# Rebuilding the first layer norm of an eight-stage transformer kernel, and the order of its start

## The chip, the cores and the metric

The kernel runs on one core of a Trainium2 chip. The metric is the device time of one launch in microseconds (us), as the median of several runs; the profile is one more execution, taken with the hardware profiler.

## The reference

Eight stages work in turn on `x` (8 batches x 128 tokens x 512 numbers); each adds its result to `x` after a layer norm. There are four cross-attentions over the same context `ctx_4096` and four feed-forward networks. What the change touches is the beginning, stage 0:

```python
def _layernorm(x, axis=-1, eps=1e-05):
    m = jnp.mean(x, axis=axis, keepdims=True)
    v = jnp.var(x, axis=axis, keepdims=True)
    return (x - m) / jnp.sqrt(v + eps)
...
        x = _rmsnorm(hidden_states, ln_weight)      # x * rsqrt(mean(x*x) + EPS) * weight
        h_q = (x @ w_q.T).reshape(b, lq, H, DH)     # H = 32 heads, DH = 128
        h_k = (key_value_states @ w_k.T).reshape(b, lk, H, DH)
        h_v = (key_value_states @ w_v.T).reshape(b, lk, H, DH)
        score = jnp.einsum('bqhd,bkhd->bhqk', h_q, h_k)
        score = score + position_bias[None]
        ...
        attn = jnp.einsum('bhqk,bkhd->bqhd', score, h_v).reshape(b, lq, H * DH)
        out = attn @ w_out.T
        return hidden_states + out
...
    x = x + _L0_xattn_ref(_layernorm(x, axis=-1), ctx_4096, ...)
```

So the normalised `x` is used twice in stage 0: scaled once more by the root of its own mean square as the input of the queries, and added unscaled to `x`.

## The kernel before

All matrices are fp32 values that are split in two fp32r parts, a "high" copy and a "low" remainder, and each product is three matmuls (high x high, high x low, low x high; `PASSES`). The context is held transposed as `ctxT[:, 0 or 1, chunk, token]`, the normalised activations as `xnT` in the same form, with 1024 tokens and four chunks of 128 features. Weights come in tiles of 128x512 (256 KB) through a ring of four slots, `ring`, and are split into `w_kv`, `w_kv2`, `w_in` and `w_out`. POOL makes both parts (L651 high, L653 low).

Each engine runs its own instruction list, in the order in which it is written out; semaphores tie them together. Stage 0 runs 32 heads in 8 groups of 4; group 0 and the last group are written out, the six between are a loop (`Fori`). The attentions of stages 4 (`LA[2]`) and 6 (`LA[3]`) have such loops too.

The start of the kernel, before any loop:

- SP queues (`start_sp`) the constants, half of `x` (batches 0 to 3, 1 MB), four 256 KB pieces of the context into the ring, the other half of `x`, the mask, and four more context pieces, each of which has to wait until POOL has split an earlier piece out of the same ring slot. Only then come two loads for a later stage (`F0_b`) and the first weights: key, value, value, query of head 0, key and query of head 1 (`attention_sp`).
- ACT copies each context piece to the high part (L2163), POOL subtracts for the low part (L2170), 8 pieces each.
- DVE (`dve_tail(dve, 0, None)`) takes the statistics of each batch (L437, L439). After four batches it computes the reciprocal root of the variance by Newton steps (`dve_rsqrt`, L409 to L419, 11 tiny operations) and then a second root for the mean square. This chain of some 26 operations runs twice, once for each half of the batches (`dve_ln_rstd`). It then norms each batch in three passes (`dve_ln_norm`): L467 subtracts the mean and scales, L471 adds the result to `x`, L473 scales by the second root. Four buffers (`tbuf`, `pbuf`) hold normed batches.
- PE turns a normed batch (four 128x128 transposes, L484) into one of four banks, ACT copies it out (L494), and DVE makes the low part (L507).
- PE's own order is: turns of batches 0 to 3, keys of head 0 (two halves of 12 matmuls of 128x512), values of the pair of heads 0 and 1 (four fills of 24 matmuls of 128x256, alternating between the banks `proj0` and `proj1`), turns 4 to 7, queries of head 0 (two halves), scores, keys and queries of head 1, and then the steady order of group 0. ACT empties `proj0` (L952), DVE empties `proj1` (L955).

Ahead of stage 4's attention DVE executes 32 waits on a semaphore that was reached long before (`DVE_ALIGN`, L2269).

Of the kernel before, what the change touches and what calls it, by code (L numbers as in the profile page):

```python
# [7 lines left out]
F32 = mybir.dt.float32  # L8
# [19 lines left out]
DVE_ALIGN = 32  # L28
# [228 lines left out]
def build(nc, ins, out):  # L257

    with ExitStack() as ctx:
# [61 lines left out]
        with nc.sbuf_tensor("low_a2", [P, 11 * 96], F32R) as low_a2, nc.sbuf_tensor("low_b2", [96, D], F32R) as low_b2:  # L321
# [22 lines left out]
        ctx_split = sem("ctx_split")  # L344
# [3 lines left out]
        ln_stats, ln_moments, ln_shifted, ln_newton, ln_rstd, ln_normed, ln_full, ln_high, ln_low, ln_rms, ln_kept = (  # L348
            sem(f"ln_{n}") for n in "stats moments shifted newton rstd normed full high low rms kept".split())
# [77 lines left out]
        ln_calls = [0]  # L427
        LN_STAGES = [0, 1, 3, 4, 5, 6, 7]
# [4 lines left out]
        def dve_ln_stats(dve, n, b):  # L433

            if n == 0 and b % BH == 0:
                dve.wait_ge(x_landed[b // BH], 16)
            dve.bn_stats(stats[:, b, :], x[:, b, :]).then_inc(ln_stats, 1)  # L437
            dve.wait_ge(ln_stats, 8 * n + b + 1)
            dve.bn_aggr(moments[:, b, :], stats[:, b, :]).then_inc(ln_moments, 1)  # L439

        def dve_ln_rstd(dve, n, half):
# [7 lines left out]
            if n == 0:  # L449

                dve.scalar_tensor_tensor(rrms[:, cols], rstd[:, cols], 1.0, rstd[:, cols], ALU.mult,
                                         ALU.mult).then_inc(ln_rms, 1)
                dve.wait_ge(ln_rms, 3 * half + 1)
                dve.tensor_tensor(rrms[:, cols], rrms[:, cols], moments[:, cols, 1], ALU.mult).then_inc(ln_rms, 1)
                dve.wait_ge(ln_rms, 3 * half + 2)
                dve.tensor_scalar(nw_v[:, cols], rrms[:, cols], EPS, None, ALU.add).then_inc(ln_rms, 1)
                dve.wait_ge(ln_rms, 3 * half + 3)
                dve_rsqrt(dve, rrms[:, cols], nw_v[:, cols], nw_t[:, cols], ln_shifted, ln_newton, ln_calls[0])
                ln_calls[0] += 1

        def dve_ln_norm(dve, n, b):
# [6 lines left out]
            if n == 0:  # L468
                norm.then_inc(ln_kept, 1)
                dve.wait_ge(ln_kept, 2 * b + 1)  # L470
                dve.tensor_tensor(x[:, b, :], x[:, b, :], out_ap, ALU.add).then_inc(ln_kept, 1)  # L471
                dve.wait_ge(ln_kept, 2 * b + 2)
                dve.tensor_scalar(out_ap, out_ap, rrms[:, b:b + 1], None, ALU.mult).then_inc(ln_normed, 1)  # L473
            else:
                norm.then_inc(ln_normed, 1)
# [11 lines left out]
        def act_ln_high(act, n, b):  # L487
# [4 lines left out]
            if n == 0:  # L492
                for c in range(DC):
                    a = act.activation(xnT[:, 0, c, b * S:(b + 1) * S], src[:, c, :], ACT.Copy,  # L494
                                       scale=vecs[:, V_LNW + c:V_LNW + c + 1])
            else:
                a = act.activation(xnT[:, 0, :, b * S:(b + 1) * S], src, ACT.Copy)
            a.then_inc(ln_high, 1)

        def dve_ln_low(dve, n, b):  # L500
# [4 lines left out]
            if n == 0:  # L505
                for c in range(DC):
                    a = dve.scalar_tensor_tensor(xnT[:, 1, c, b * S:(b + 1) * S], src[:, c, :],  # L507
                                                 vecs[:, V_LNW + c:V_LNW + c + 1],
                                                 xnT[:, 0, c, b * S:(b + 1) * S].bitcast(F32), ALU.mult, ALU.subtract)
            else:  # L510
                a = dve.tensor_tensor(xnT[:, 1, :, b * S:(b + 1) * S], src, xnT[:, 0, :, b * S:(b + 1) * S].bitcast(F32),  # L511
                                      ALU.subtract)
            a.then_inc(ln_low, 1)
# [26 lines left out]
        def pe_tail(pe, n, out_of):  # L540
            for b in range(B):
                if out_of:
                    out_of(b)
# [7 lines left out]
            for A in LA.values():  # L551
                if A.stage == n:
                    if n == 0:
                        pe.wait_ge(ctx_split, 8)
                    for what in "kv":
                        project_head(pe, A, 0, 0, what)
# [23 lines left out]
        def dve_tail(dve, n, add_of):  # L580
# [3 lines left out]
            early = BH if add_of else BH - 1  # L584
            for b in range(B):
                if add_of:
                    add_of(b)
# [27 lines left out]
        def attention_sp(sp, A):  # L615
# [20 lines left out]
            for what, _, j in A.first:  # L636
                load(0, j, what)
            group(0)
# [4 lines left out]
        def attention_pool(pool, A):  # L643
# [130 lines left out]
        def project_values(pe, A, g, j):  # L774
# [4 lines left out]
            for fill in range(4):  # L779
# [8 lines left out]
        def project_head(pe, A, g, j, what, squares=None):  # L788
# [11 lines left out]
            for half in range(2):  # L800
# [188 lines left out]
        def attention_act(act, A):  # L989
# [65 lines left out]
            exps(0, 0, 1)  # L1055
            if A.normed:
# [27 lines left out]
        def attention_dve(dve, A):  # L1084
# [75 lines left out]
            def add(p, b):  # L1160
                m.wait(dve, "added", B * p + (b - B + 1))
# [982 lines left out]

        def start_sp(sp):
            sp.dma_start(consts[:, :], ins["consts"]).then_inc(consts_landed, 16)
            sp.dma_start(vecs[:, :], ins["vecs"]).then_inc(consts_landed, 16)
            for n in range(8):
                if n % 4 == 0:
                    sp.dma_start(x[:, n:n + 4, :], ins["x"][:, n:n + 4, :]).then_inc(x_landed[n // 4], 16)  # L2150
                if n == 4:
# [227 lines left out]
```

## Time and profile before

| | |
|---|---|
| median of 3 runs | 3134.81 us (3134.13 to 3142.85) |
| the profiled execution, device time | 3132.72 us |
| its span, first to last instruction | 3130.9 us |
| PE busy, share of the span | 94% |
| mean granted TensorE clock | 0.982 |
| matmuls | 16224 |

In the rows below "PE" is the matmul side of TensorE, "PEld" its weight loads, DVE VectorE, ACT ScalarE, POOL GpSimd, SPq the queue of SyncE that issues transfers. A line such as L388 is a line of the kernel. Brackets at the end of a timeline row give the idle time of the engine before the row, and what ended it. A busy matmul row has a modelled end, so rows of PE can overlap a little.

### The profile page before, as it was taken

How to read it: one execution, taken by the hardware profiler on the slowest of the kernel's cores; microseconds unless marked ns; L12 is line 12 of the kernel's file. 1: busy time of each engine (PE TensorE's matmuls, PEld its weight loads, DVE VectorE, ACT ScalarE, POOL GpSimd, SP SyncE). 2: the span in 40 equal slices, each digit the busy share in tenths (PEclk: the TensorE clock that was granted, in tenths of full speed). 3: DMA queues.
4: the chain of work that ended last, by engine and by line, in shares of the span. 5: the costliest groups of instructions: out<-in, count | busy, mean ns of one | idle time of the engine just before them, and what ended most of it. 6: DMA issues, size and time to landing. Idle time of an engine off the chain costs nothing.

```text
span 3130.9 us, 47838 instructions
## 1 busy us (share of the span) xinstructions
PE 2952.5 (94%) x16224; PEld 2501.3 (80%) x16224; DVE 1794.2 (57%) x3625; ACT 1038.1 (33%) x3466; POOL 991.2 (32%) x842
## 2 busy tenths in 40 slices
PE   4999999999989989889989999999889999999899
PEld 4788888888877857768778888888768888888687
DVE  7454444444462258878766666666774444544744
ACT  2222222222222217622144444444313333333332
POOL 3424233333313236533331333222213333332221
PEclk9999999999999999989999999999999999999999
DMA  2111111111111110011110111001011111110111
GB/s 90 58 40 47 39 46 39 46 30 51 40 35 54 33 35 29 26 32 39 42 35 21 34 33 33 27 24 33 24 34 38 39 41 38 33 33 20 44 47 44
DMA packets 69141, 119.75 MB, mean 38 GB/s; under 512 B 8745, under 2 KB 14249, under 8 KB 68641
## 3 DMA queue, kind: packets, MB, share of 16 engines
q1 hardware_dynamic: 69026, 118.26, 12.6%
q8 instruction: 67, 1.10, 0.1%
q14 instruction: 48, 0.39, 0.0%
HBM read 116.06 MB, written 2.10 MB: 38 GB/s over the span
## 4 chain that ended last, share of the span: by engine, by line
PE 82%; DVE 11%; ACT 3%; issue 2%; DMA 0%; DVEq 0%; ACTq 0%; SPq 0%
PE proj L388 39%; PE outp L388 22%; PE heado L905 6%; PE score L872 4%; PE turn L892 2%; PE score L388 2%; DVE stats L437 1%; PE outp L1789 1%; DVE x L1163 1%; PE score L1374 1%; DVE xnT L511 1%; ACT sq L1000 1%; ACT tbuf L1012 1%; PE heado L1789 1%; ACT acts L1033 1%
## 5 line engine op out<-in xcount | busy, mean ns | idle before, releaser
L388 PE MATMUL outp<-w_out,acts 128*128 128x512 f32 x3288 | 847.7, 403 | 20.8 <-DVE x L1163 12.3
L388 PE MATMUL proj<-xnT,w_in 128*128 128x512 f32 x3288 | 783.7, 394 | 8.4 <-DVE xnT L511 2.7
L388 PEld LDWEIGHTS proj<-xnT,w_in 128*128 128x128 f32 x3288 | 613.2, 189 | 139.1 <-issue 6.0
L388 PEld LDWEIGHTS outp<-w_out,acts 128*128 128x128 f32 x3288 | 600.9, 190 | 149.4 <-DVE x L1163 17.4
L388 PE MATMUL proj<-ctxT,w_kv 128*128 128x512 f32 x1536 | 368.7, 396 | 5.8 <-ACT big L952 5.1
L1163 DVE TENSOR_TENSOR x<-x,outp 128x512 f32<-128x512 f32 x384 | 260.9, 684 | 189.1 <-PE outp L388 187.3
L651 POOL TENSOR_TENSOR w_out<-ring,consts 128x512 fp32r<-128x512 f32 x96 | 102.0, 1063 | 840.5 <-PE outp L388 840.5
L388 PEld LDWEIGHTS proj<-ctxT,w_kv 128*128 128x128 f32 x1536 | 285.4, 189 | 71.5 <-ACT big L952 9.4
L955 DVE COPY big<-proj 128x512 f32<-128x512 f32 x136 | 93.6, 689 | 361.7 <-PE proj L388 361.5
L651 POOL TENSOR_TENSOR w_kv<-ring,consts 128x512 fp32r<-128x512 f32 x96 | 100.4, 1046 | 486.8 <-DMA ring<-in_L_wk 463.2
L1187 DVE TENSOR_TENSOR acts<-heado,acts 128x512 fp32r<-128x512 f32 x192 | 132.8, 691 | 175.2 <-ACT acts L1033 175.2
L905 PEld LDWEIGHTS heado<-ptbuf,big 128*128 128x128 f32 x1536 | 201.5, 192 | 30.7 <-ACT ptbuf L1031 15.8
L1033 ACT ACTIVATE acts<-heado 128x512 fp32r<-128x512 f32 x192 | 115.1, 599 | 325.0 <-PE heado L905 325.0
L905 PE MATMUL heado<-ptbuf,big 128*128 128x128 f32 x1536 | 205.1, 277 | 12.5 <-ACT ptbuf L1031 7.2
L952 ACT ACTIVATE big<-proj 128x512 f32<-128x512 f32 x136 | 80.6, 593 | 401.8 <-PE proj L388 400.3
L1031 ACT ACTIVATE ptbuf<-turn 128x512 f32<-128x512 f32 x192 | 114.4, 596 | 267.8 <-PE turn L892 267.8
L388 PE MATMUL proj<-w_kv,ctxT 128*128 128x256 f32 x1536 | 188.9, 284 | 6.6 <-DVE big L955 6.6
L388 PEld LDWEIGHTS proj<-w_kv,ctxT 128*128 128x128 f32 x1536 | 187.7, 191 | 8.4 <-DVE big L955 7.2
L872 PEld LDWEIGHTS score<-big 128*128 128x128 f32 x1536 | 183.2, 192 | 9.0 <-issue 4.4
L872 PE MATMUL score<-big 128*128 128x128 f32 x1536 | 187.2, 275 | 3.0 <-issue 1.7
L1510 DVE TENSOR_TENSOR x<-x,outp 128x512 f32<-128x512 f32 x168 | 115.2, 686 | 105.9 <-PE outp L388 105.6
L651 POOL TENSOR_TENSOR w_in<-ring,consts 128x512 fp32r<-128x512 f32 x96 | 106.6, 1111 | 158.2 <-PE proj L388 157.8
(248 smaller groups left out, 4049.1 us busy)
## 6 DMA issues: line engine op xcount, KB each, us to landing
ring<-in_L_wq SPq DMA_DIRECT2D x96, 256.0 KB, 2.7
ring<-in_L_wo SPq DMA_DIRECT2D x96, 256.0 KB, 2.7
ring<-in_F_in SPq DMA_DIRECT2D x52, 256.0 KB, 2.7
ring<-in_L_wk SPq DMA_DIRECT2D x48, 256.0 KB, 2.7
ring<-in_L_wv SPq DMA_DIRECT2D x48, 256.0 KB, 3.3
ring<-in_F_out SPq DMA_DIRECT2D x41, 256.0 KB, 2.6
x<-in_x SPq DMA_DIRECT2D x2, 1024.0 KB, 7.4
ring<-in_ctxT SPq DMA_DIRECT2D x8, 256.0 KB, 4.8
```

What stands on the lines that cost most here:

```text
L388: mm = pe.matmul(bank_ap, w_ap(a, c), rhs(b, c), start=first and c == 0 and n == 0, stop=last and c == chunks - 1 and n == len(PASSES) - 1)
L651: pool.tensor_tensor(dst[:, slot, 0, :], ring[:, r, :], zeros512, ALU.add).then_inc(m["high_w"], 1)
L872: mm = pe.matmul(score[half][:, b * P:(b + 1) * P], qT[:, t], kT[:, t], start=True, stop=True)
L892: mm = pe.transpose(turn[:, b * P:(b + 1) * P], probs[j % 2][:, half, b * P:(b + 1) * P], ident)
L905: mm = pe.matmul(heado[:, b * P:(b + 1) * P], v_pair[:, n, j % 2, :] if A.own_kv else v[:, n * S:(n + 1) * S], ptbuf[:, half, b * P:(b + 1 ...
L952: return engine.activation(dst, src, ACT.Copy)
L955: return engine.tensor_copy(dst, src)
L1031: act.activation(ptbuf[:, half, :], turn[:, :], ACT.Copy).then_inc(m["tfree"], 1)
L1033: act.activation(acts[:, j, 0, half * HALF:(half + 1) * HALF], heado[:, :], ACT.Copy)\
L1163: dve.tensor_tensor(x[:, b, :], x[:, b, :], outp[b % 2][:, :], ALU.add).then_inc(m["added"], 1)
L1187: dve.tensor_tensor(acts[:, j, 1, cols], heado[:, :], acts[:, j, 0, cols].bitcast(F32), ALU.subtract)\
L1510: dve.tensor_tensor(x[:, b, :], x[:, b, :], outp[b % 2][:, :], ALU.add).then_inc(m["added"], 1)
```

## The change

The start is written anew, in four functions of its own (`start_sp`, `start_pe`, `start_act`, `start_dve`), and the special cases for stage 0 leave the shared layer-norm helpers.

- The context goes to a free buffer (`big`) in four loads of 512 KB that wait for nothing; both halves of `x` and the first weights are queued right behind, the `F0_b` loads and the mask after weights. POOL splits five of the eight context pieces, DVE three.
- ACT makes the high parts of the first three weight tiles (key, value, value), which POOL did.
- The two roots are computed once for all eight batches, with their work tiles in a PSUM bank (`outp[0]`). The two scalings are multiplied into one, so a norm is one pass: even batches on DVE, odd ones on ACT, into eight buffers. The turns use six banks.
- `x = x + norm(x)` becomes one ACT pass for each batch (`x * keep + shift`), behind the exponentials of the first scores; the first additions to `x` (L1163) wait for it.
- PE does keys, value fill 0, turns 0 to 3, fill 1, turns 4 and 5, fill 2, turns 6 and 7, fill 3, queries.
- A tiny ACT operation ahead of the first copies brings the activation table load forward. The 32 waits ahead of stage 4 leave.

```diff
-            for _ in range(DVE_ALIGN):
-                dve.wait_ge(consts_landed, 32)
...
             def split(g, j, what, dst, slot):
...
-                m.wait(pool, ("landed", r), 16 * A.landing(g, j, what))
-                pool.tensor_tensor(dst[:, slot, 0, :], ring[:, r, :], zeros512, ALU.add).then_inc(m["high_w"], 1)
+                if not (A.own_kv and isinstance(g, int) and g == 0 and (what, 0, j) in A.first[:3]):
+                    m.wait(pool, ("landed", r), 16 * A.landing(g, j, what))
+                    pool.tensor_tensor(dst[:, slot, 0, :], ring[:, r, :], zeros512, ALU.add).then_inc(m["high_w"], 1)
...
             exps(0, 0, 1)
+            if A.own_kv:
+                act.wait_ge(ln_rms, 7)
+                for b in range(B):
+                    act.activation(x[:, b, :], x[:, b, :], ACT.Identity, bias=nw_t[:, b:b + 1], scale=nw_v[:, b:b + 1])\
+                       .then_inc(ln_kept, 1)
...
             def add(p, b):
+                if A.own_kv and isinstance(p, int) and p == 0:
+                    dve.wait_ge(ln_kept, b + 1)
...
+        CTX_POOL, CTX_DVE = (0, 1, 2, 4, 6), (3, 5, 7)
...
         def start_sp(sp):
             sp.dma_start(consts[:, :], ins["consts"]).then_inc(consts_landed, 16)
             sp.dma_start(vecs[:, :], ins["vecs"]).then_inc(consts_landed, 16)
+            sp.dma_start(x[:, 0:BH, :], ins["x"][:, 0:BH, :]).then_inc(x_landed[0], 16)
+            for n in range(4):
+                sp.dma_start(big[:, n, :], ins["ctxT"][:, n, :]).then_inc(ctx_landed[n], 16)
+            sp.dma_start(x[:, BH:B, :], ins["x"][:, BH:B, :]).then_inc(x_landed[1], 16)
+
+        def start_pe(pe):
...
+            pe.wait_ge(ctx_split, len(CTX_POOL))
+            pe.wait_ge(ctx_split_dve, len(CTX_DVE))
+            project_head(pe, A, 0, 0, "k")
+            project_values(pe, A, 0, 0, fills=[0])
+            for b in range(4):
+                turn_first(b)
+            project_values(pe, A, 0, 0, fills=[1])
+            for b in range(4, 6):
+                turn_first(b)
+            project_values(pe, A, 0, 0, fills=[2])
+            for b in range(6, 8):
+                turn_first(b)
+            project_values(pe, A, 0, 0, fills=[3])
+
+        def start_act(act):
...
+            for r, dst in enumerate((w_kv[:, 0, 0, :], w_kv[:, 1, 0, :], w_kv2[:, 1, 0, :])):
+                A.events.wait(act, ("landed", r), 16)
+                act.activation(dst, ring[:, r, :], ACT.Copy).then_inc(A.events["high_w"], 1)
+            take_projection(act, True, A, 0, 0, "k")
+            norm_first(1)
+            norm_first(3)
+            high_first(0)
+            take_values_fill(act, True, A, 0, 0, 0)
+            high_first(1)
+            norm_first(5)
+            norm_first(7)
+            for b in range(2, 6):
+                high_first(b)
+            take_values_fill(act, True, A, 0, 0, 2)
+            for b in range(6, 8):
+                high_first(b)
...
+            mean, var = moments[:, :, 0], moments[:, :, 1]
+            arg, work = outp[0][:, 0:B], outp[0][:, B:2 * B]
+            dve.wait_ge(ln_moments, B)
+            dve.tensor_scalar(arg, var, EPS, None, ALU.add).then_inc(ln_rstd, 2)
+            dve.wait_ge(ln_rstd, 2)
+            dve_rsqrt(dve, rstd[:, :], arg, work, ln_shifted, ln_newton, 0)
+            dve.tensor_tensor(work, rstd[:, :], rstd[:, :], ALU.mult).then_inc(ln_rms, 1)
...
+            dve_rsqrt(dve, rrms[:, :], arg, work, ln_shifted, ln_newton, 1)
+            keep, shift = nw_v, nw_t
+            dve.tensor_tensor(rrms[:, :], rrms[:, :], rstd[:, :], ALU.mult).then_inc(ln_rms, 1)
...
+            dve.scalar_tensor_tensor(shift[:, :], rrms[:, :], -1.0, mean, ALU.mult, ALU.mult).then_inc(ln_rms, 1)
...
+            norm_first(0)
+            norm_first(2)
+            take_projection(dve, False, LA[0], 0, 0, "k")
+            norm_first(4)
+            norm_first(6)
...
+            for b in range(2):
+                low_first(b)
+            take_values_fill(dve, False, LA[0], 0, 0, 1)
+            for b in range(2, 7):
+                low_first(b)
+            take_values_fill(dve, False, LA[0], 0, 0, 3)
+            low_first(7)
```

## Rows read from the trace of the kernel before

**Rows 1.** The page: busy shares, and the chain that ended last.

```profile
PE 2952.5 (94%) x16224; PEld 2501.3 (80%) x16224; DVE 1794.2 (57%) x3625; ACT 1038.1 (33%) x3466; POOL 991.2 (32%) x842
...
PE 82%; DVE 11%; ACT 3%; issue 2%; DMA 0%; DVEq 0%; ACTq 0%; SPq 0%
```

**Rows 2.** Waits, 0 to 90 us: total us, times, longest.

```profile
PE turn L484 <- DVE tbuf L473: 26.1, 1, 26.1
```

**Rows 3.** Timeline of the start: start us, us, engine, line, what.

```profile
7.91 0.70 DVE L437 BATCH_NORM_STATS2 stats<-x 128x6 f32<-128x512 f32 x1 [4.36 <-DMA x<-in_x]
8.62 1.28 ACT L2163 ACT_TABLE_LOAD   x1 [8.62 <-DMA ring<-in_ctxT]
...
11.23 0.76 DVE L445 TENSOR_SCALAR nw_v<-moments 128x4 f32<-128x4 f32 x1
...
24.18 0.55 DVE L467 TENSOR_SCALAR tbuf<-x,moments,rstd 128x512 f32<-128x512 f32 x1
...
27.24 1.14 ACT L494 ACTIVATE xnT<-turn,vecs 128x128 fp32r<-128x128 f32 x4 [8.00 <-PE turn L484]
...
37.44 6.84 PE L388 MATMUL proj<-ctxT,w_kv 128*128 128x512 f32 x24
...
43.05 0.16 DVE L445 TENSOR_SCALAR nw_v<-moments 128x4 f32<-128x4 f32 x1
...
44.12 3.03 PE L388 MATMUL proj<-w_kv,ctxT 128*128 128x256 f32 x24
...
48.20 0.55 DVE L467 TENSOR_SCALAR tbuf<-x,moments,rstd 128x512 f32<-128x512 f32 x1
...
52.35 10.87 PE L388 MATMUL proj<-w_kv,ctxT 128*128 128x256 f32 x72 [5.20 <-DVE big L955]
...
63.05 0.60 PE L484 MATMUL turn<-consts,tbuf 128*128 128x128 f32 x4
...
64.72 3.01 PE L388 MATMUL proj<-xnT,w_in 128*128 128x512 f32 x12
...
69.24 3.00 PE L388 MATMUL proj<-xnT,w_in 128*128 128x512 f32 x12 [1.51 <-DVE xnT L507]
...
73.18 2.02 PE L872 MATMUL score<-big 128*128 128x128 f32 x16 [0.94 <-DVE big L955]
...
91.92 0.60 ACT L952 ACTIVATE big<-proj 128x512 f32<-128x512 f32 x1 [6.17 <-PE proj L388]
```

**Rows 4.** Busy us of PE, PEld, DVE, ACT, POOL; granted clock, DMA share, GB/s.

```profile
8.00:12.00 4.00, 0.00 (x0) 0.00 (x0) 3.82 (x9) 3.37 (x5) 1.31 (x2) 1.00 1.02 399
50.00:56.00 6.00, 3.65 (x17) 3.65 (x18) 5.49 (x10) 0.00 (x0) 0.00 (x0) 0.51 0.01 3
```

**Rows 5.** Transfers, 0 to 90 us: KB each, median us from issue to landing.

```profile
ring<-in_L_wk SPq DMA_DIRECT2D x3, 256.0 KB, 2.8
...
consts<-in_consts SPq DMA_DIRECT2D x1, 181.5 KB, 2.3
...
vecs<-in_vecs SPq DMA_DIRECT2D x1, 47.0 KB, 2.2
```

**Rows 6.** Groups of one line: duration in ns, min/median/max, then first and last start.

```profile
L417 DVE SCALAR_TENSOR_TENSOR heado<-heado,rq x96: 173/173/175, 1596.8 to 2232.0; 128x8 f32<-128x8 f32 x96
L417 DVE SCALAR_TENSOR_TENSOR nw_t<-nw_t,rstd x48: 161/161/1190, 15.7 to 2940.8; 128x4 f32<-128x4 f32 x48
...
L467 DVE TENSOR_SCALAR pbuf<-x,moments,rstd x28: 515/538/1257, 29.1 to 2942.5; 128x512 f32<-128x512 f32 x28
...
L2170 POOL TENSOR_TENSOR ctxT<-ring,ctxT x8: 1263/1264/1267, 10.7 to 19.5; 128x512 fp32r<-128x512 f32 x8
L653 POOL TENSOR_TENSOR w_kv<-ring,w_kv x4: 1287/1328/1591, 28.1 to 38.8; 128x512 fp32r<-128x512 f32 x4
...
L953 ACT ACTIVATE big<-proj,vecs x48: 689/690/704, 2331.3 to 2887.3; 128x512 f32<-128x512 f32 x48
```

**Rows 7.** Transfer queues, 1820 to 2120 us, inside stage 4's loop: packets, MB, share.

```profile
q1 hardware_dynamic: 5040, 9.18, 10.3%
```

More of the change, by code:

```diff
@@ L27 @@
 NPAIR = NH // 2
-DVE_ALIGN = 32
 EPS = 1e-5
@@ L347, in build @@
         kqn_made = sem("kqn_made")
-        ln_stats, ln_moments, ln_shifted, ln_newton, ln_rstd, ln_normed, ln_full, ln_high, ln_low, ln_rms, ln_kept = (
-            sem(f"ln_{n}") for n in "stats moments shifted newton rstd normed full high low rms kept".split())
+        ln_stats, ln_moments, ln_shifted, ln_newton, ln_rstd, ln_normed, ln_full, ln_high, ln_low, ln_rms, ln_act_normed, ln_kept = (
+            sem(f"ln_{n}") for n in "stats moments shifted newton rstd normed full high low rms act_normed kept".split())
         out_landed = sem("out_landed")
@@ L427, in build @@
         ln_calls = [0]
+        first_normed = normed + [ptbuf[:, 0, :], ptbuf[:, 1, :]] + \
+            [maskadd[:, BH * i:BH * i + BH, :].rearrange("p b n -> p (b n)") for i in range(2)]
+        first_banks = ln_banks + outp
         LN_STAGES = [0, 1, 3, 4, 5, 6, 7]
@@ L491, in act_ln_high @@
             src = ln_banks[b % 4][:, :].rearrange("p (c t) -> p c t", c=DC)
[L492 to L498, printed above, removed]
+            act.activation(xnT[:, 0, :, b * S:(b + 1) * S], src, ACT.Copy).then_inc(ln_high, 1)
         def dve_ln_low(dve, n, b):
@@ L583, in dve_tail @@
             turned = n in LN_STAGES
-            early = BH if add_of else BH - 1
+            early = BH
             for b in range(B):
-                if add_of:
-                    add_of(b)
+                add_of(b)
                 if n > 7:
@@ L634, in group @@
                     load(n + ahead, j, what)
-            for what, _, j in A.first:
+            for n, (what, _, j) in enumerate(A.first):
                 load(0, j, what)
+                if A.own_kv and n == 2:
+                    sp.dma_start(mask_bytes[:, :], ins["mask0"]).then_inc(mask_landed, 16)
+            if A.own_kv:
+                sp.dma_start(sq[:, :], ins["F0_b"][:, 0:T]).then_inc(b_landed, 16)
+                sp.dma_start(ring[:, 4, 0:11 * P - T], ins["F0_b"][:, T:11 * P]).then_inc(b_landed, 16)
             group(0)
@@ L772, in rms_call, with project_values @@
             return 5 * g + (0 if what == "k" else j + 1)
-        def project_values(pe, A, g, j):
+        def project_values(pe, A, g, j, fills=range(4)):
             m = A.events
@@ L778, in project_values @@
             m.wait(pe, "split", A.tile(g, j + 1, "v") + 1)
-            for fill in range(4):
+            for fill in fills:
                 half = fill % 2
@@ L786, in project_values, with project_head @@
                 mm.then_inc(m["pfull", half], 1)
-        def project_head(pe, A, g, j, what, squares=None):
+        def project_head(pe, A, g, j, what, squares=None, halves=(0, 1)):
             m = A.events
@@ L799, in project_head @@
             m.wait(pe, "split", A.tile(g, j, what) + 1)
-            for half in range(2):
+            for half in halves:
                 m.wait(pe, ("pfree", half), n)
@@ new lines, in start_dve @@
+            dve.wait_ge(x_landed[1], 16)
+            for b in range(BH, B):
+                dve_ln_stats(dve, 0, b)
+            mean, var = moments[:, :, 0], moments[:, :, 1]
[5 more added lines that the diff above has]
+            dve.tensor_tensor(work, rstd[:, :], rstd[:, :], ALU.mult).then_inc(ln_rms, 1)
```

118 lines of the change are left out of this document (61 added, 57 removed).

## The prediction

> **What bounds the kernel now.** The page comes first: PE is busy 94% of the span, the chain that ended last lies 82% on PE, and the rest of it is mostly DVE [rows 1]. Nearly everywhere, then, only less work or less waiting on PE can save time. The list of waits for the first 90 us shows one stretch where PE does nothing: 26.1 us until the first normed batch exists [rows 2]. The timeline of that stretch gives the order of events [rows 3]. `x` lands at 7.9 us, DVE takes the statistics of four batches until 11.23, and then needs until 24.18 for the 26 tiny root operations, 12.95 us. The same 26 operations for the other four batches run from 43.05 to 48.20, 5.15 us. What differs is POOL, which subtracts context pieces during the first. The keys start at 37.44, the first value fill at 44.12, then DVE is late with emptying `proj1` (its root chain and norms stand ahead of that copy) and PE stands still for 5.2 us up to 52.35. The clock falls: 0.51 granted from 50 to 56 us, which is the lower level, 1.2 GHz, after the stop [rows 4]. The remaining 72 matmuls take 10.87 us where three fills at 3.03 would take 9.09, so 1.8 us more go there. The query projection ends at 69.24 + 3.00 = 72.24, and the scores start at 73.18. From there the order of the program is the old one. So the change is worth what it takes from the 72.24 us, unless something behind it gives time back.
>
> **The change part by part.** I work out when each input of PE is there, and then let PE run its own order.
>
> *Transfers.* In the old kernel 181.5 + 47 KB of constants [rows 5], 1024 KB of `x` and 256 KB of context were in SBUF at 8.62 us [rows 3], and the stretch 8 to 12 us moved 399 GB/s [rows 4]. Now 2048 KB of context, 1024 KB of `x`, 64 KB of bias and the 256 KB key tile are queued without a wait. Up to and with the key tile that is 3136 KB more than had landed at 8.62, which is 8.0 us at 399 GB/s: the second half of `x` lands near 15.9 and the key tile near 16.7. The two value tiles follow 0.7 us apart. SP queues all of this without a wait, so the data, not SP, is the limit. The mask and the `F0_b` loads are behind the weights, with tens of us to spare. The key and query tiles of head 1 still wait for POOL's splits and for a landing (2.8 us); nobody needs them before the scores.
>
> *Context and key split.* Context pieces land from about 9.2 to 13.2 us. ACT's table load is out of the way by then. POOL has five pieces at 1.26 us [rows 6], from about 10 on, so to 16.3 or, with DVE's three splits in between, 17.2. The key tile: 16.7 landed, 0.6 us ACT copy, 1.33 us POOL low part: 18.6. **PE starts the keys at 18.7** instead of 37.44.
>
> *Root chain.* DVE has its splits behind it at some 16.4, takes four statistics (3.3 us as between 7.91 and 11.23 in [rows 3]) and starts the roots at 19.7. There are 28 operations; at the undisturbed pace (5.15 us for 26, 0.2 each) that is 5.5 us, so 25.2. POOL is busy all through with weight tiles. What this does depends on where the operands are: L417 with its work tile in SBUF ranges from 161 to 1190 ns, the same line with it in PSUM from 173 to 175 in all of its 96 places [rows 6], with POOL busy 32% of the span [rows 1]. The new chain has its work tiles in PSUM; three of its operations still have two inputs in SBUF and can each lose up to 1.03 us. That gives 25.2 to 28.3; I take 27.0, since POOL is hardly ever free. The first norm costs 0.54 us, up to 1.26 beside POOL [rows 6]: 28.0. ACT norms batches 1 and 3 beside it.
>
> *PE's order.* Keys 6.84 us (I keep the slow beginning of the old row, as PE is idle before it here too) to 25.5; fill 0, 3.03, to 28.6; the first turn finds its batch, by a margin of 0.6. Eight turns at 0.42 (four from 63.05 to 64.72) are 3.3, three more fills 9.1, two query halves 6.0. If all three root operations and both norms lose the full amount, the second norm is there at 30.8 and the copy that frees `proj1` at 31.5 instead of 30.3, a stop of 1.2 us. I put 0.6 for it. Sum: 6.84 + 12.12 + 3.3 + 6.0 + 0.6 = 28.9, so the queries end at 18.7 + 28.9 = **47.6 us**. Other inputs are in time: ACT needs 1.14 us for a turned batch [rows 3] and has the last one copied near 41, DVE's last low part is there near 43.7, and the second query half starts near 44.6. DVE's mask work, three operations, fits before the queries end.
>
> *Sum.* 72.24 - 47.6 = 24.6 us less.
>
> *What comes behind.* ACT's eight passes over `x` stand between the exponentials of head 0 and the next copy. The old kernel has 6.17 us of idle there [rows 3]. One pass is like L953, 0.69 us with one pointer operand [rows 6], less some 0.1 of overlap: 4.8 to 5.5 us. Hidden, with 0.7 us to spare, and PE wouldn't wait at once if it weren't. The Trainium skill (ScalarE: Activation LUTs, What ACT_TABLE_LOAD costs) says that each pointer operand adds about 93 ns, and these passes have two; by it the eight take an estimated 5.6 us, still hidden, and no run of the kernel before shows such an operation. DVE's waits in L1163 are met long before. Of the three high parts that POOL loses, 3.1 us, nothing counts by itself; it brings the key split forward and is in the 18.6. The 32 waits ahead of stage 4 stand where DVE waits for PE anyway: nothing.
>
> The profiled execution took 3132.7 us, so it becomes 3108.1. The median of the runs is 2.1 above the profiled time: **3110**.
>
> **The rivals.**
>
> *B: the norms stay late.* The root chain doesn't get free of POOL, by these three operations or by PSUM operands that lose time too, or the transfers come slower than 399 GB/s. If the operations behind 19.7 go at the pace of the first chain (12.95 us for 26, so some 14 for 28) the first norm is there near 34.5, PE stops for about 6 us in front of its turns, and the stop brings the lower clock level again, 1.8 us as above. Gain 17: 3118. For it: POOL has eight weight operations to do in this stretch. Against it: the two L417 rows.
>
> *C: given back.* The start gets shorter but something behind holds the end, so the time is 3125 to 3135. ACT's `x` passes are the only new work there, and 6.17 us cover them; the loops have PE at 94% and more. I find no place for it.
>
> *D: slower.* The change moves all later DVE code: the start loses a root chain and norm passes, L1163 gains eight waits, the 32 leave, so stage 4's loop begins some 50 instructions earlier. In 300 us of that loop the queues show only data, no packet of code [rows 7]; it runs from what is loaded. If at its new place it didn't fit, DVE would fetch a piece again in every round and stand still. The nearest row for such a piece is the 47 KB load, 2.2 us to landing [rows 5]; with up to three pieces in each of six rounds, all on the path, 40 us. It decides against the change from 34 us on (24.6 and the 9.4 of a measurable loss), that is at 5.7 us a round, nearly the whole 6.6: 3110 + 40 = 3150. With one piece a round it is 13 us: 3123. The Trainium skill (Runtime: NRT & Kernel Launch, Instruction fetch mechanics) speaks for such a stall: a taken branch whose target is outside the two loaded pages forces a fetch before execution can continue. The trace neither shows one nor how near the old place was to it.
>
> *E: it does not do what it says.* The old and new start cost the same to 0.3%, since PE needs the late query weights or another input that I put too early. That needs 15 us of new waiting; the weights would have to land at 30 us.
>
> **How the numbers follow.** The forecast, 23 to 26.5 us less, has 0.62, its own range is 3107 to 3113. B has 0.24 (3113 to 3120), C and E together 0.06, D 0.04 with a small (faster, 3117 to 3125) and 0.02 with a large price; 0.02 are left for a gain above 27. The median itself has moved up to 8 us between runs of the kernel before, mostly under 1. Range: 3104 to 3121. The bound of what can be told is 0.3%, 9.4 us: faster 0.92, within 0.05, slower 0.03.
>
> **What would show each step right or wrong.** The first key matmul at 18 to 19.5 us, not later than 21. L2163's copies begin at 9 to 9.5. L409 to L419 in the start at 0.17 us each, not 1.2, with a POOL operation beside them. The first L484-like turn directly behind value fill 0, with under 1.5 us of idle before it. No stretch at clock 0.5 between 25 and 50 us. The scores of head 0 at 48 to 49.5 instead of 73.18. ACT's `x` passes under 5.8 us in all, and PE's idle time between them and 110 us as before. No code packet in the loop of stage 4. The prediction fails if PE still waits several us ahead of its turns, if the key weights land after 20, or if the stages from 100 us on take longer than before.

## The result, and the profile after

The changed kernel takes 3109.39 us (median of 5 runs, 3106.46 to 3117.8) against 3134.81 us (5 runs of before, 3133.76 to 3144.47): ratio 0.9919, interval 0.9906 to 0.9932, so it is faster, by 0.8%. The forecast was 3110 us with a range of 3104 to 3121. The profiled execution took 3107.48 us, with a span of 3105.7 us; 3108.1 was forecast for its time. The executions fall into two groups, which move a median by up to 9 us with their number: of ten executions of the changed kernel, these five and five later ones, six took 3106.5 to 3109.7 us at a mean granted clock of 0.983 to 0.985, and four 3116.5 to 3117.8 at 0.980 or 0.981, and the kernel before has three at 3133.8 to 3134.8 and two at 3142.9 and 3144.5.

The page of the changed kernel, its busy shares, its chain and the queue q14, which carries packets of code, beside [rows 1]:

```profile
PE 2946.2 (95%) x16224; PEld 2496.9 (80%) x16224; DVE 1775.8 (57%) x3586; ACT 1046.8 (34%) x3482; POOL 984.4 (32%) x836
...
q14 instruction: 47, 0.38, 0.0%
...
PE 83%; DVE 10%; ACT 3%; issue 2%; POOL 0%; DMA 0%; DVEq 0%; SPq 0%; ACTq 0%; POOLq 0%
```

The matmuls are as many as before. PE is busy 6.3 us less (2946.2 against 2952.5), and the span is 25.2 us shorter, so some 19 of the 25 us came from waiting, and the other 6 are less busy time for the same number of matmuls. The list of PE's waits up to 60 us, the answer to [rows 2]:

```profile
PE proj L387 <- POOL w_kv L623: 18.3, 1, 18.3
PE score L842 <- DVE big L925: 0.9, 1, 0.9
```

The 26.1 us ahead of the first turn are now 18.3 us ahead of the first key matmul, and nothing stops PE between the keys and the scores. The timeline of the start, in the order of [rows 3]:

```profile
0.74 1.28 ACT L2177 ACT_TABLE_LOAD   x1 [0.74 <-PEq L2455]
7.28 0.69 DVE L437 BATCH_NORM_STATS2 stats<-x 128x6 f32<-128x512 f32 x1 [3.71 <-DMA x<-in_x]
8.64 4.92 ACT L2180 ACTIVATE ctxT<-big 128x512 fp32r<-128x512 f32 x8 [5.04 <-DMA big<-in_ctxT]
9.42 7.51 POOL L2202 TENSOR_TENSOR ctxT<-big,ctxT 128x512 fp32r<-128x512 f32 x5 [8.97 <-ACT ctxT L2180]
15.85 1.99 ACT L2183 ACTIVATE w_kv<-ring 128x512 fp32r<-128x512 f32 x3 [2.28 <-DMA ring<-in_L_wk]
16.90 3.73 POOL L623 TENSOR_TENSOR w_kv<-ring,w_kv 128x512 fp32r<-128x512 f32 x3
18.30 8.48 PE L387 MATMUL proj<-ctxT,w_kv 128*128 128x512 f32 x24 [18.30 <-POOL w_kv L623]
19.13 0.17 DVE L2223 TENSOR_SCALAR outp<-moments 128x8 f32<-128x8 f32 x1
24.45 0.92 DVE L2234 TENSOR_TENSOR rrms<-rrms,rstd 128x8 f32<-128x8 f32 x1
25.40 0.97 DVE L2236 SCALAR_TENSOR_TENSOR nw_t<-rrms,moments 128x8 f32<-128x8 f32 x1
26.29 0.54 DVE L2239 TENSOR_SCALAR tbuf<-x,moments,rrms 128x512 f32<-128x512 f32 x1
26.63 3.03 PE L387 MATMUL proj<-w_kv,ctxT 128*128 128x256 f32 x24
29.49 0.60 PE L2144 MATMUL turn<-consts,tbuf 128*128 128x128 f32 x4
41.57 5.61 PE L387 MATMUL proj<-xnT,w_in 128*128 128x512 f32 x24
48.13 2.02 PE L842 MATMUL score<-big 128*128 128x128 f32 x16 [0.95 <-DVE big L925]
```

The root chain runs from 19.13 to 26.37, 28 operations in 7.2 us; in [rows 3] 26 of them took 12.95. The first norm is ready at 26.8, 2.7 us ahead of its turn at 29.49. The scores start at 48.13 instead of 73.18, 25.05 us earlier, and the span is 3130.9 - 3105.7 = 25.2 us shorter. What the start gained arrived at the end whole.

ScalarE behind the first scores, the eight passes over `x` and the next copy:

```profile
60.61 5.74 ACT L1029 ACTIVATE x<-x,nw_t,nw_v 128x512 f32<-128x512 f32 x8
...
66.89 0.60 ACT L922 ACTIVATE big<-proj 128x512 f32<-128x512 f32 x1 [0.54 <-PE proj L387]
```

They took 5.74 us and left 0.54 us of the 6.17 idle us of [rows 3].

### The profile page after: what moved, and what is told of

Same layout as the page of the kernel before. It is cut to its first block, busy times and chain, and to the rows that moved or that the text cites. A ratio compares the mean times of both kernels' runs of the same rounds, so it can differ in the third digit from the quotient of the medians.

```text
span 3105.7 us, 47797 instructions
## 1 busy us (share of the span) xinstructions
PE 2946.2 (95%) x16224; PEld 2496.9 (80%) x16224; DVE 1775.8 (57%) x3586; ACT 1046.8 (34%) x3482; POOL 984.4 (32%) x836
## 4 chain that ended last, share of the span: by engine, by line
PE 83%; DVE 10%; ACT 3%; issue 2%; POOL 0%; DMA 0%; DVEq 0%; SPq 0%; ACTq 0%; POOLq 0%
PE proj L387 39%; PE outp L387 22%; PE heado L875 6%; PE score L842 4%; PE turn L862 3%; PE score L387 2%; DVE stats L437 1%; PE outp L1766 1%; PE score L1351 1%; DVE x L1140 1%; DVE xnT L480 1%; ACT sq L970 1%; ACT tbuf L982 1%; PE heado L1766 1%; ACT acts L1003 1%
## 5 line engine op out<-in xcount | busy, mean ns | idle before, releaser
L387 PE MATMUL proj<-ctxT,w_kv 128*128 128x512 f32 x1536 | 370.3, 397 | 25.0 <-POOL w_kv L623 18.3
```

The lines of the kernel that those rows point to most:

```text
L387: mm = pe.matmul(bank_ap, w_ap(a, c), rhs(b, c), start=first and c == 0 and n == 0, stop=last and c == chunks - 1 and n == len(PASSES) - 1)
```

## The experiments

**1. The work tiles in SBUF again** (`roots_sbuf`, one run).

```diff
-            arg, work = outp[0][:, 0:B], outp[0][:, B:2 * B]
+            arg, work = nw_v[:, :], nw_t[:, :]
```

> The changed kernel, with the two work tiles of the root chain in SBUF instead of PSUM. Theory (what a root operation loses depends on whether its operands lie in SBUF while POOL works): the 28 operations, 6.3 us in the changed kernel (19.13 to about 25.4 without the last one's wait), take about 1.2 us each as long as POOL is busy with weight tiles, so about 12 us; the first turn moves from 29.5 to about 34 us, PE stops for some 5 us before it, and the first scores move from 48.1 to 52 to 55. Rival (the split of the work and the single chain make the difference, not the place of the tiles): chain within 1 us of before, first scores at 48 to 49.

Measured: 3112.34 us, span 3110.6; keys at 18.98, scores at 51.11. Its timeline, root operations on DVE and the first turn:

```profile
20.12 1.20 DVE L408 TENSOR_SCALAR nw_t<-nw_v 128x8 int32<-128x8 int32 x1
21.36 0.96 DVE L410 TENSOR_SCALAR rstd<-nw_t 128x8 int32<-128x8 int32 x1
22.36 0.17 DVE L414 TENSOR_TENSOR nw_t<-rstd,nw_v 128x8 f32<-128x8 f32 x1
22.56 1.13 DVE L416 SCALAR_TENSOR_TENSOR nw_t<-nw_t,rstd 128x8 f32<-128x8 f32 x1
...
28.69 0.17 DVE L2226 TENSOR_TENSOR nw_t<-rstd 128x8 f32<-128x8 f32 x1
...
32.40 0.66 PE L2144 MATMUL turn<-consts,tbuf 128*128 128x128 f32 x4 [2.48 <-DVE tbuf L2239]
```

Up to 28.5 us most operations take about 1 us and end with an operation of POOL: that of 21.36 ends at 22.32, POOL's of 21.25 at 22.29. The one of 22.36 falls between two operations of POOL and takes 0.17. From 28.5 on POOL is through with its weights and every one takes 0.17. The chain lasts 12.2 us instead of 7.2, and PE stops for 2.48 us. So PSUM work tiles are worth 5 us of chain, of which 2.7 would have been slack of the first turn anyway. Rival B's mechanism is real, and at its full size it would have cost 2.5 us and not 6. The expectation had the chain right (about 12 us) and the stop and the first scores too late (5 us, 52 to 55), since the keys take 8.07 us here.

**2. Turns ahead of the keys** (`turns_first`, one run): the keys and value fill 0 go behind turn 3, in PE's and in ACT's order.

```diff
+            for b in range(4):
+                turn_first(b)
             project_head(pe, A, 0, 0, "k")
             project_values(pe, A, 0, 0, fills=[0])
-            for b in range(4):
-                turn_first(b)
```

> The changed kernel, with the turns of batches 0 to 3 back in front of the keys and value fill 0, and ACT's copies in the matching order. Theory (PE's order hides the root chain): PE waits for the first norm until about 26.8 us, so the keys start near 29 instead of 18.3 and the first scores near 57 to 59 instead of 48.1, that is 9 to 11 us given back of the 25. Rival (the gain is in the earlier inputs, the order is worth little): first scores before 52.

Measured: 3118.43 us, span 3116.6. PE waits 27.54 us for the first norm, the keys start at 30.84 and the scores at 57.40, 9.3 us later than with the new order. So of the 25 us some 9 hang on PE's order alone: it hides the root chain behind the keys and the first fill.

**3. Only the root work tiles changed, in the kernel before** (`before_psum_roots`).

```diff
+            arg, work = (outp[0][:, 0:B], outp[0][:, B:2 * B]) if n == 0 else (nw_v, nw_t)
...
-                dve.scalar_tensor_tensor(rrms[:, cols], rstd[:, cols], 1.0, rstd[:, cols], ALU.mult,
-                                         ALU.mult).then_inc(ln_rms, 1)
+                dve.tensor_scalar(work[:, cols], rstd[:, cols], 1.0, None, ALU.mult)\
+                   .then_inc(ln_rms, 1)
+                dve.wait_ge(ln_rms, 4 * half + 1)
+                dve.tensor_tensor(work[:, cols], work[:, cols], rstd[:, cols], ALU.mult).then_inc(ln_rms, 1)
```

> The kernel before, with one part of the change alone: the work tiles of stage 0's two root chains in a PSUM bank instead of SBUF (one small copy is added to each chain). Theory (the first chain takes 12.95 us for 26 operations because its SBUF tiles collide with POOL's context pieces): the first chain takes 5.3 to 6.5 us, the first turn comes near 19.5 instead of 26.1; but the weights are only split at 29.5, so the keys move less than that, from 37.4 to 30 to 32, and the whole kernel gains 4 to 7 us. Rival (the chain is hidden behind the weights and the transfers anyway): the first chain is shorter and the first scores stay within 2 us of 73.2.

Measured: 3125.63 us (6 runs, 3124.19 to 3127.83), ratio to before 0.9971, interval 0.9959 to 0.9984. The chain runs from 11.6 to 17.0, 5.4 us instead of 12.95, and the scores start at 65.36, 7.8 us earlier. Its timeline keeps the second stop of before:

```profile
20.80 1.09 PE L487 MATMUL turn<-consts,tbuf 128*128 128x128 f32 x4 [20.80 <-DVE tbuf L476]
...
29.90 8.43 PE L388 MATMUL proj<-ctxT,w_kv 128*128 128x512 f32 x24 [1.21 <-POOL w_kv L656]
...
45.02 10.36 PE L388 MATMUL proj<-w_kv,ctxT 128*128 128x256 f32 x72 [3.83 <-DVE big L958]
```

A third of the gain, then, is the operands' place alone; expected were 4 to 7 us of the whole time, and the median is 8.8 under that of the kernel before in the same set (3134.42). Stage 4's loop plays no part in it: PE is busy 290.22 of the 300 us from 1820 on, against 289.39 before.

**4. All eight context pieces split by POOL** (`ctx_pool_only`, one run).

```diff
-        CTX_POOL, CTX_DVE = (0, 1, 2, 4, 6), (3, 5, 7)
+        CTX_POOL, CTX_DVE = tuple(range(8)), ()
...
-            pe.wait_ge(ctx_split_dve, len(CTX_DVE))
```

> The changed kernel, with all eight context pieces subtracted by POOL, none by DVE. Theory (the key split queues behind the context pieces on POOL, and it releases PE at 18.3): eight pieces at 1.26 to 1.5 us from 9.4 on end near 20, the key tile's low part near 21.5, so the keys start 2.5 to 3.5 us later than 18.3, and the statistics and the roots come up to 2 us earlier, which helps nobody. First scores 50.5 to 51.5. Rival (the transfers set the start, POOL has room): keys start before 19.5.

Measured: 3110.67 us, span 3108.9. The keys start at 21.18, 2.9 us later, and the scores at 50.34, 2.2 later, since the keys take 7.80 us instead of 8.48. The first low part of a key tile is what PE waits for, and POOL's queue sets it.

**5. The high parts by POOL** (`highs_on_pool`, one run).

```diff
-                if not (A.own_kv and isinstance(g, int) and g == 0 and (what, 0, j) in A.first[:3]):
+                if True:
...
-                act.activation(dst, ring[:, r, :], ACT.Copy).then_inc(A.events["high_w"], 1)
```

> The changed kernel with the high parts of the first three weight tiles made by GpSimd again, before their low parts, and not by ScalarE. GpSimd has 3 more operations of about 1.2 us in front of the key tile's low part. Theory (the low part of the first key tile on GpSimd is what the keys wait for): the keys begin 1 to 2.5 us later than 18.30, at 19.3 to 20.8, and everything to the first scores moves by the same (49 to 50.6 instead of 48.13); span 1 to 2.5 us longer. Rival (the wait is for the tile's transfer): keys begin within 0.5 us of 18.3.

Measured: 3106.50 us, span 3104.7. The keys start at 19.46, 1.2 us later than 18.30, as the theory has it; they take 7.86 us, so the scores come at 48.68, 0.55 later. The span isn't longer but 1.0 shorter. POOL's high part of the key tile (1.03 us from 16.94 on) is what stands ahead of its low part; the other two come behind it. So this part is worth a microsecond at the keys, and less than single executions scatter by: the two profiles of the changed kernel had their scores at 48.13 and 47.45, and six of its ten executions span 3104.7 to 3107.9 us. That it helps the end is not shown.

**6. All norms by DVE** (`norms_dve_only`, one run): `norm_first` for batches 0 to 3 and 4 to 7 on DVE, none on ACT, and PE waits for `ln_normed` alone.

```diff
-                pe.wait_ge((ln_normed, ln_act_normed)[b % 2], b // 2 + 1)
+                pe.wait_ge(ln_normed, b + 1)
...
-            norm_first(0)
-            norm_first(2)
+            for b in range(4):
+                norm_first(b)
```

> The changed kernel, with all eight first norms on DVE, none on ACT. Theory (sharing is worth little, since PE has keys and a value fill to do while the norms are made): batch 3 is normed about 1.5 to 2.5 us later, the copy that frees the second projection bank moves from 28.2 to 30 or 31, PE waits 0 to 1.5 us before value fill 1, first scores at 48 to 50. Rival (DVE is the bound of this stretch): first scores at 52 or later.

Measured: 3120.68 us, span 3118.9, with a mean granted clock of 0.979, and with 0.84 between 2200 and 2330 us, where the changed kernel has 0.95; that is far from the edit, so its total says nothing of it. Locally the keys start at 19.07, fill 0 and the turns follow without a wait, the first turn at 30.10 (11.03 us after the keys; 11.19 in the changed kernel), the scores at 48.76 (29.69 after the keys; 29.83). Norms shared by two engines gave PE nothing here.

**7. The passes over `x` in quarters** (`x_pass_quarters`, one run).

```diff
-                    act.activation(x[:, b, :], x[:, b, :], ACT.Identity, bias=nw_t[:, b:b + 1], scale=nw_v[:, b:b + 1])\
-                        .then_inc(ln_kept, 1)
+                    for c in range(DC):
+                        a = act.activation(x[:, b, c * P:(c + 1) * P], x[:, b, c * P:(c + 1) * P], ACT.Identity,
+                                           bias=nw_t[:, b:b + 1], scale=nw_v[:, b:b + 1])
+                    a.then_inc(ln_kept, 1)
```

> The changed kernel with ScalarE's eight passes over x (x times scale plus bias, between two score passes) cut into 32 quarter passes of 128x128, same work. In the changed kernel the eight took 5.74 us in a gap between two ScalarE tasks of about 6.3 us. Theory (the passes cost nothing only while they fit that gap): 32 small passes at 0.3 to 0.4 us take 9.5 to 12.5 us, so ScalarE's next copy of the first queries' turn is 3 to 6 us late; TensorE shows a wait of 2 to 5 us between 60 and 80 us that the changed kernel doesn't have, and the span is longer by that. Rival (there is slack behind the gap, rival C's cover is wider than the gap): no new wait on TensorE over 0.5 us and a span within 1 us of the changed kernel's.

Measured: 3112.73 us, span 3110.9. Its timeline behind the first scores:

```profile
60.97 12.43 ACT L1030 ACTIVATE x<-x,nw_t,nw_v 128x128 f32<-128x128 f32 x32
...
73.28 0.59 ACT L922 ACTIVATE big<-proj 128x512 f32<-128x512 f32 x1
...
74.02 8.04 PE L387 MATMUL proj<-xnT,w_in 128*128 128x512 f32 x24 [4.10 <-ACT big L922]
```

The passes take 6.7 us more and the copy is 6.4 us late. PE stops for 4.1 us, where it doesn't stop in the changed kernel. The granted clock then reads 0.50 from 74 to 78 us, and the 24 matmuls behind the stop take 8.04 us instead of 5.61. The span is 5.2 us longer. The cover is about as wide as forecast, and rival C had this place: with passes of twice the length it would have been a fifth of the gain.

**8. No waits ahead of stage 4's loop, in the kernel before** (`before_no_pads`).

```diff
-DVE_ALIGN = 32
+DVE_ALIGN = 0
```

> The kernel before, without the 32 waits ahead of stage 4, nothing else. Theory (the waits cost nothing and the place of the later loops costs nothing): the same time as the kernel before within 0.3%, and no packet of code while stage 4's loop runs. Rival D of the prediction (the place of the code decides): code packets in every round of stage 4's loop or a later one, and 5 to 40 us more.

Measured: 3145.31 us (6 runs, 3142.83 to 3146.17), ratio to before 1.0039, interval 1.0026 to 1.0052. Slower by some 12 us, so the expectation was wrong. The stretch 1820 to 2120 us, inside stage 4's loop, as in [rows 7]:

```profile
q1 hardware_dynamic: 4740, 8.63, 10.6%
q14 instruction: 16, 0.13, 0.2%
```

Where before shows only data, there are 16 packets of 8 KB of code. They come in bursts of four within 6 us, 87 us apart, with a single one between two bursts. That is five for each of the five returns to the head of a loop of six rounds, and 25 in all: the whole execution has 73 where before has 48. DVE's waits from 1700 to 2200 us have a row that before doesn't have:

```profile
DVE pbuf L1107 <- issue: 18.4, 5, 3.8
```

DVE stands still five times, for 3.6 to 3.8 us each, waiting for nothing that the profile shows, and each time a burst of code packets begins within these microseconds. The profile doesn't name the engine that q14 serves; that these packets are DVE's is read from its stops. That is rival D's mechanism, in the kernel before with one constant changed.

**9. 64 waits put back into the changed kernel** (`waits_64`).

```diff
+            for _ in range(64):
+                dve.wait_ge(consts_landed, 32)
```

> The changed kernel, with 64 idle waits (stored two to an instruction, so 32 instructions) ahead of stage 4's attention on DVE. Counted in the compiled programs, stage 4's loop of 272 DVE instructions begins at instruction 1736 in the kernel before (72 behind a multiple of 128), 1720 (56) in that kernel without its 32 waits, where the loop fetched 4 packets of 8 KB of code in every round and cost 12 us, and 1689 (25) in the changed kernel. Here it begins at 1721 (57). Theory (the place of the loop alone decides, and a packet is 128 instructions): 4 code packets a round again, 9 to 13 us more than the changed kernel, so 3118 to 3123 us. Rival (the 12 us belong to leaving the waits out, for their timing): the same time as the changed kernel, 3107 to 3112, since here there are more waits, not fewer.

Measured: 3122.51 us (10 runs, 3120.53 to 3134.75), ratio to before 0.9967, interval 0.9957 to 0.9977, so 13 us of the gain are lost. The profiled execution is the longest of the ten, 3134.75 us; like that of `norms_dve_only` it has a low granted clock between 2200 and 2330 us (0.86 where the changed kernel has 0.95), which lies behind the loop. Queues and busy times (PE, PEld, DVE, ACT, POOL, then clock, DMA share, GB/s) of the same stretch, 1820 to 2120 us, in this kernel:

```profile
q14 instruction: 19, 0.16, 0.2%
...
1820.00:2120.00 300.00, 283.03 (x1603) 241.13 (x1602) 183.77 (x527) 124.44 (x573) 82.63 (x70) 0.99 0.11 31
```

and in the changed one, where the queues show data alone:

```profile
1820.00:2120.00 300.00, 289.92 (x1650) 247.94 (x1649) 189.48 (x542) 126.39 (x579) 82.72 (x70) 1.00 0.11 31
```

PE is busy 6.9 us less in 300 us. A round lasts about 87 us, so that is 2.0 us a round. `before_no_pads` has 283.79 in its stretch against 289.39 of before, 1.6 us a round. From 1700 to 2200 us, which holds all five returns, PE is busy 9.8 us less here and 9.2 us less there; these are most of the 12 to 13 us, and the rest isn't located. DVE's stops are the same as in `before_no_pads`: five, 18.0 us in all.

What may decide can be counted in the compiled kernels: the loop has 272 instructions for DVE, and it begins at DVE's instruction 1736 before and 1689 after, where nothing is fetched, and at 1720 and 1721 in the two that fetch. The waits' own time isn't what costs: taking them away hurt one kernel and adding them hurt the other. Which places are bad isn't shown. If a packet holds 128 instructions, as the expectation takes it, a loop of 272 lies in three or in four such pieces. But with boundaries at the multiples of 128 in this count all four loops lie in three (they begin 25, 56, 57 and 72 instructions behind one), and five packets a return are neither three nor four. No run moved the start step by step.

**10. PE kept at work ahead of the keys** (`warm`): 36 transposes into a bank that nobody reads, when the second part of the context has landed.

```diff
+            pe.wait_ge(ctx_landed[1], 16)
+            for _ in range(36):
+                pe.transpose(score[0][:, 0:P], ident, ident)
```

> The changed kernel, with 36 idle transposes of the identity on PE between the landing of the second context load and the keys, written to a bank that is free then. The keys took 8.48 us in the changed kernel, 5.7 to 5.9 for the same 24 matmuls later. Theory (the first matmuls are slow because TensorE's clock is at its lower level after idling): the keys take 5.7 to 6.5 us and the first scores come 2 to 2.8 us earlier, if the root chain (first norm ready at 26.8) lets them: then PE waits for the norm, and the gain is 1.5 to 2.8 us, hardly measurable in the median (0.1%). Rival (the keys are slow for another reason, as late operands): keys at 8.3 to 8.6 us as before.

Measured: 3106.62 us (5 runs, 3106.04 to 3107.98), ratio to before 0.9916, interval 0.99 to 0.9931; span 3104.2. Its timeline:

```profile
10.08 6.10 PE L2149 MATMUL score<-consts 128*128 128x128 f32 x36 [10.08 <-DMA big<-in_ctxT]
...
18.43 5.71 PE L387 MATMUL proj<-ctxT,w_kv 128*128 128x512 f32 x24 [2.25 <-POOL w_kv L623]
```

The keys take 5.71 us instead of 8.48, and the scores start at 46.29, 1.84 us earlier.

PE's matmuls, the granted clock, the share of the DMA engines and GB/s, in steps of 2 us within the keys:

```profile
18.50:20.50 2.00, 2.00 (x9) 1.00 0.40 123
20.50:22.50 2.00, 2.00 (x11) 1.00 0.72 238
22.50:24.50 2.00, 2.00 (x13) 1.00 0.66 256
```

**11 and 12. Both once more, on one chip** (`after_again` and `warm_again`).

> The changed kernel itself once more, unchanged, beside the one below on the same chip. All theories: 3106 to 3112, 0.9915 to 0.993 of before.

> The changed kernel with 36 idle 128x128 transposes on TensorE ahead of the keys, unchanged from its first run. Theory (the keys lose 2.8 us because TensorE comes to them idle): profiled span 1 to 2.5 us under that of the changed kernel in this call, median 1 to 3 us under. Rival (the first run's gain was chance): median within 0.5 us of it.

Measured: 3116.49 us (5 runs, 3107.36 to 3117.76; ratio to before 0.9937, 0.9923 to 0.995) for the changed kernel, and 3106.55 us (4 runs, 3103.62 to 3106.79; ratio 0.9908, 0.9893 to 0.9923) for `warm`. The changed kernel missed its expectation of 3106 to 3112: three of its five executions took 3116.5 to 3117.8. So the 9.9 us between these medians are not the effect of the edit alone; the profiled spans, 3105.8 and 3104.6, differ by 1.2, in the range the theory gave. The keys took 7.73 and 7.31 us, 0.42 apart where the first pair had 2.77. The same columns as above from 18.5 us on, first the changed kernel's first profile:

```profile
18.50:20.50 2.00, 2.00 (x5) 1.00 0.58 137
20.50:22.50 2.00, 2.00 (x6) 1.00 0.88 254
22.50:24.50 2.00, 2.00 (x6) 1.00 0.57 224
24.50:26.50 2.00, 2.00 (x10) 1.00 0.03 12
```

then `warm_again`:

```profile
18.50:20.50 2.00, 2.00 (x8) 0.80 0.48 131
20.50:22.50 2.00, 2.00 (x6) 0.50 0.97 285
22.50:24.50 2.00, 2.00 (x9) 0.85 0.53 207
24.50:26.50 2.00, 2.00 (x15) 1.00 0.02 4
```

In `warm_again` the clock fell to the lower level, 1.2 GHz, within the keys, after the 2.85 us in which PE had nothing between the transposes and the keys; in `warm`, 2.25 us of idle, it did not fall. At the lower level it did 6 matmuls in 2 us. The changed kernel does 5 and 6, the same pace, although its column reads 1.00. The trace settles this. Its first record of the clock lies at 24.2 us, and ahead of it the column prints 1.00 without a record. The key matmuls start 0.43 us apart up to 24.0 us and 0.23 us apart from 24.3 us on; in `warm_again` they are 0.43 apart where the record is the lower level and 0.23 elsewhere. The second profile of the changed kernel has its first record at 22.7 us, with the same change of pace there, and keys of 7.73 us. So 14 of the 24 key matmuls run at the pace of the lower level, and the transposes take that away in one execution and only partly in the other. The transfers aren't the cause: in `warm` they are about as dense in the same 6 us, with POOL as busy, at 9 to 13 matmuls in 2 us.

The nine executions of `warm` and `warm_again` lie between 3103.6 and 3108.0 us, the ten of the changed kernel between 3106.5 and 3117.8. The two medians with the transposes, both 3106.6, are about 1 us under 3107.5, the median of the six shorter executions of the changed kernel. How much of the rest is the edit's doing is open.

## Why the prediction was right

*Transfers and splits.* Keys forecast at 18.7, measured 18.30, and 18.38 in the second profile. The term held, though not by the path that I gave. I had the key tile's transfer land last, at 16.7, with POOL free by then; ACT starts to copy the landed tile at 15.85, and POOL is at its context pieces until 16.9. Experiments 4 and 5 show that POOL's queue sets the start: 2.9 us for three more context splits, 1.2 for the high part of the key tile. The number is near because POOL was through within the 16.3 to 17.2 that I gave it, 0.4 us ahead of the 17.3 at which I had the tile landed and copied.

*Root chain.* Forecast 25.2 to 28.3, taken 27.0, measured 26.37. Two of the three operations with two inputs in SBUF lost 0.75 and 0.80 us (L2234, L2236), the third nothing. Operations with a work tile in PSUM took 0.17 throughout, with POOL busy 1.9 of every 2 us. The first turn's margin was 2.7 us and not 0.6: the first norm was ready 1.2 us earlier than forecast, and the turn came 0.9 later, since the keys took longer.

*PE's order.* Here a term was mis-sized. The keys were put at 6.84 us, from the row of before; they took 8.48. What the row of before hides is the clock: the first record of before lies at 39.9 us, and 6 of its 24 key matmuls are 0.43 us apart, where the changed kernel has 14. In before PE had done four turns ahead of them, in the new kernel nothing at all; but `before_psum_roots` had the same four turns ahead and took 8.43 us, with its first record at 35.7, so the turns alone don't decide it. The stop of 0.6 that I added didn't occur. Sum of keys, fills, turns and queries: 28.9 forecast, 47.18 - 18.30 = 28.9 measured. The errors cancel: from one group's start to the next, +1.5 at the keys, -0.6 for the stop, -0.9 in fills, turns and queries. That they cancel is luck; without it the total would have been off by 1 to 2 us, still inside the range.

*The passes over `x`.* Forecast 4.8 to 5.5 us, measured 5.74. The estimate from the Trainium skill (ScalarE: Activation LUTs, What ACT_TABLE_LOAD costs), 5.6 us with its 93 ns for each of two pointer operands, was nearer than my row with one pointer. The step held because 6.17 us covered either; experiment 7 shows what lay beyond.

*The 32 waits: "nothing".* This step was wrong as a step. Their place is a matter of 12 to 13 us, half of the gain, and the kernel got by because the new start happens to put the loop at a harmless place. The trace of before couldn't show it. Rival D named the mechanism and, at one piece a round, "13 us: 3123"; `waits_64` took 3122.5. That the totals agree is partly luck. I priced a piece by one transfer of 2.2 us, one to three of them in each of six rounds. Measured are five packets at each of five returns, which stop DVE for 3.7 us and cost PE about 2. At this price D takes half of the gain and doesn't turn it into a loss. The rule of the Trainium skill (Runtime: NRT & Kernel Launch, Instruction fetch mechanics), that a taken branch out of the two loaded pages has to fetch, has the stall right: DVE's five stops of `before_no_pads` agree with it. These runs also show packets of 8 KB, and the same loop of 272 instructions without a stop at other places.

*Behind the start.* "Nothing behind the start gives time back" held: 25.05 us at the scores, 25.2 in the span. No clock level below 1.00 shows between 25 and 50 us in either profile of the changed kernel, where before has 0.51 after its stop [rows 4]; with the stop gone, so is the fall.

*Where the gain comes from.* Kept apart by experiment: the order of PE 9.3 us (2), root work tiles 7.8 in the old order (3) but 2.3 in the new (1, counted from the keys to the scores), context pieces for DVE 2.2 (4), high parts by ACT up to 0.6 (5), norms on two engines 0 (6). These overlap and don't add up to 25. Not tried alone were the loads that no longer wait for the ring, the single root chain for all eight batches, the norm in one pass and the move of `x = x + norm(x)` to ACT; what is left belongs to them together.

## What to carry to other kernels

A kernel that can't start its main engine before its inputs are there should give it first what needs the least preparation, and let the longest chain of small operations run beside that. An edit that adds or removes instructions on an engine with a run-time loop moves the loop: look for code packets in the loop's stretch of the trace afterwards, and for idle time of that engine that nothing released. Here 32 idle waits were worth half of what the edit gained. A cost row of a matmul group holds the clock of its place; ahead of the first record of the clock it is read from the distance between two matmuls, not from the column.

## What the runs showed of the hardware that wasn't expected

- The place of a loop in an engine's code costs about 2 us a round here, with nothing in any instruction's own duration to tell of it: only five packets of code a return, five stops of DVE of 3.4 to 3.8 us put down to "issue", and 5.6 and 6.9 us less PE work in 300.
- Tiny DVE operations (128x8) with all operands in SBUF took 0.96 to 1.20 us while POOL was at work, ending with its operation, and 0.17 when it wasn't or between two of its operations; with the work tile in PSUM 0.17 beside POOL as well, with two inputs in SBUF 0.17 to 0.97.
- Matmuls of 128x512 started 0.43 us apart in the first 5.7 us after 18 us of idle and 0.23 apart later, while the column of the granted clock printed 1.00: the first record of the clock lies at 24.2 us.
